# A two-row-block network on one core: the derived forms of h2 in three parts on VectorE, x transposed half a step earlier, a shorter Newton step

## The reference

```python
h  = s4d(log_dt, C=x, B, inv_A_real, A_imag, 1024)             # (32, 128, 1024)
h  = h  + layernorm(h)  @ attn_weight.T + attn_bias             # called h2 below
h2 = layernorm(h)
base = h2 @ W.T + b                                            # 1024 -> 1024
gates = softmax(h2 @ Wr.T)                                     # 4 experts
proj  = h2 @ A.T                                               # 4 experts x rank 8
out = h + base + sum over e of 2 * gates[e] * (proj[e] @ Bm[e].T)
```

## Time and profile before

| what | value |
|---|---|
| median of 3 runs | 901.78 us |
| the profiled execution, its own time | 901.64 us |
| its span (first to last instruction) | 899.7 us |
| TensorE (PE) busy | 85% of the span |
| VectorE (DVE) busy | 79% |
| ScalarE (ACT) busy | 66% |
| GpSimd (POOL) busy | 13% |

### The profile page before, as it was taken

How to read it: one execution, slowest core, us unless ns; L and a number is a source line. 1 busy time by engine, 2 the same in 40 slices (tenths; PEclk the granted TensorE clock), 3 DMA queues, 4 the chain that set the end, 5 groups by cost and what they waited for, 6 DMA issues and landing times.

```text
span 899.7 us, 15024 instructions
## 1 busy us (share of the span) xinstructions
PE 765.4 (85%) x5166; PEld 370.9 (41%) x5166; DVE 709.4 (79%) x1291; ACT 596.7 (66%) x979; POOL 118.3 (13%) x94
## 2 busy tenths in 40 slices
PE   2779999454989899898989899898989899898977
PEld 2624444222434344443434344343434344343433
DVE  7899996885987878787987878787987878787353
ACT  6778775665867677685777677685877677684120
POOL 2000202222020200202020200202020200202020
PEclk9979999886999999999989989899999999898999
DMA  8879676285243452526243452526243352526342
GB/s 295 247 143 172 148 160 130 72 186 101 51 93 82 83 111 50 123 50 141 54 95 77 82 111 50 122 50 140 55 91 81 82 111 50 117 50 129 51 93 62
DMA packets 258074, 94.21 MB, mean 105 GB/s; under 512 B 245424, under 2 KB 250416, under 8 KB 257912
## 3 DMA queue, kind: packets, MB, share of 16 engines
q1 hardware_dynamic: 257944, 93.66, 49.5%
q10 hardware_dynamic: 96, 0.13, 0.1%
HBM read 18.26 MB, written 16.78 MB: 39 GB/s over the span
## 4 chain that ended last, share of the span: by engine, by line
PE 43%; DVE 23%; ACT 9%; DMA 7%; issue 7%; SPq 7%; POOL 3%; DVEq 0%; POOLq 0%; ACTq 0%
PE ps_g L693 25%; PE ps_g L845 9%; PE ps_a L684 4%; DVE residual L1551 3%; DMA spare<-spare 3%; DVE u_split L1449 3%; SPq L524 2%; PE ps_x L845 2%; ACT junk L1047 2%; DVE form_tok L1879 2%; POOL form_sum L1400 2%; DVE residual L1886 2%; DMA forms<-form_tok 1%; SPq L511 1%; ACT form_tok L1230 1%
## 5 line engine op out<-in xcount | busy, mean ns | idle before, releaser
L693 PE MATMUL ps_g<-wa_hi,x 128*128 128x512 f16 x992 | 269.6, 388 | 7.3 <-DMA wa_lo<-residual 6.3
L693 PE MATMUL ps_g<-wa_lo,x 128*128 128x512 f16 x496 | 153.6, 389 | 0.0
L693 PEld LDWEIGHTS ps_g<-wa_hi,x 128*128 128x128 f16 x992 | 97.9, 100 | 130.5 <-issue 22.6
L684 PE MATMUL ps_a<-u_split,m_split 128*32 128x256 f16 x1344 | 58.1, 340 | 73.0 <-DVE u_split L1449 73.0
L845 PE MATMUL ps_g<-stage,forms 128*128 128x512 f16 x504 | 113.4, 379 | 7.1 <-DVE residual L1886 7.0
L1400 POOL TENSOR_TENSOR form_sum<-xn_b 128x512 f32<-128x512 f32 x14 | 18.1, 1290 | 581.0 <-DVE xn_b L1568 575.8
L684 PEld LDWEIGHTS ps_a<-u_split,m_split 128*32 128x32 f16 x1344 | 41.6, 117 | 92.2 <-issue 57.1
L845 PEld LDWEIGHTS ps_g<-stage,forms 128*128 128x128 f16 x504 | 48.5, 98 | 69.0 <-DVE residual L1886 9.3
L693 PEld LDWEIGHTS ps_g<-wa_lo,x 128*128 128x128 f16 x496 | 49.6, 100 | 61.8 <-issue 6.4
L1492 DVE TENSOR_TENSOR m<-x_t,q 128x512 f32<-128x512 f32 x32 | 22.0, 689 | 66.8 <-ACT x_t L1001 66.0
L1886 DVE SCALAR_TENSOR_TENSOR residual<-ps_g,unscale,residual 128x512 f32<-128x512 f32 x84 | 62.6, 745 | 14.7 <-PE ps_g L845 11.1
(11 more groups left out here) (273 smaller groups left out, 1450.2 us busy)
## 6 DMA issues: line engine op xcount, KB each, us to landing
out<-residual SPq DMA_DIRECT2D x124, 128.0 KB, 2.2
stage<-in_L_ffn_W SPq DMA_DIRECT2D x8, 512.0 KB, 14.0
x_raw<-in_x SPq DMA_DIRECT2D x38, 64.0 KB
residual<-in_L_attn_weight SPq DMA_DIRECT2D x4, 512.0 KB, 7.1
wf_hi<-in_x SPq DMA_DIRECT2D x1, 2048.0 KB, 9.4
xn_b<-in_L_ffn_W SPq DMA_DIRECT2D x4, 512.0 KB, 4.0
form_tok<-in_L_ffn_W SPq DMA_DIRECT2D x4, 512.0 KB, 5.4
forms<-form_tok SPq DMA_TRANSPOSE x106, 3.2
```

What stands on the lines that cost most here:

```text
L684: mm = pe.matmul(ps_a[q * C:(q + 1) * C, a // 2, (a % 2) * WL:(a % 2 + 1) * WL], stationary[:, q, a * C:(a + 1) * C], moving[:, q, :], sta ...
L693: mm = pe.matmul(ps[:, o, :], x1_part(part, ps is ps_g2)[:, k, :], ws[:, k, o * HALF:(o + 1) * HALF], start=k == 0 and part == 0 and ws is ...
```

## The change

Seven things are changed.

1. The four sums and differences go from GpSimd to VectorE: `add_first_form` (S1) right behind normalise_2(t, 1), `add_second_form` (S2) and `add_third_form` (S4) at the start of the next pair step, `add_fourth_form` (S3) behind its low_m. S3 is written to `form_sum`, no longer over `xn`.
2. The high parts, low parts and transposes of S2, S4 and S3 go into the next pair step. What is left at the end of a step is A22 and S1.
3. low_u(t + 1, 1) and high_u(t + 1, 1) now stand ahead of low A22 and high A22.
4. split_x(t + 2) goes ahead of square_2(t, 1), turn_x(t + 2) behind turn_x1(t + 1, 0), join_x(t + 2) ahead of phases and decays of (t + 2, 0); phases(t + 1, 1) goes ahead of square_2(t, 0).
5. `newton` has three operations, with eps multiplied by 1024 beforehand (one more operation once, at the start).
6. At the start split_x(3) and turn_x(3) go ahead of the second group of weight sums, and low_sums(3) ahead of keep_h2(2, 1).
7. At the end of the kernel the parts that were moved are written out behind the last step.

```diff
@@ SP, turn_second_forms and step
             def turn_second_forms(t):
                 turn_form(t, S1, 3, 2)
+                turn_form(t, A22, 2, 7)
+            def turn_third_forms(t):
                 turn_form(t, S2, 4, 3)
                 turn_form(t, S4, 5, 5)
-                turn_form(t, S3, 6, 6)
-                turn_form(t, A22, 2, 7)
...
             def step(t, p, stored=True, loads=True, turns=True):
-                if turns:
-                    turn_x(t + 1)
                 if stored:
                     store_pair(t - 2, 1, p)
                 if loads:
                     load_x(t + 2)
+                turn_third_forms(t - 1)
                 turn_x1(t, 1)
                 turn_pair_lora(t - 1)
+                turn_form(t - 1, S3, 6, 6)
                 turn_first_forms(t)
                 if turns:
                     turn_x1(t + 1, 0)
+                if loads:
+                    turn_x(t + 2)
                 store_pair(t - 1, 0, 1 - p)
                 turn_second_forms(t)
@@ ScalarE
                 rstd_guess(t, 1, stat_1, s_ssq1, s_log1, s_y1, m_eps)
+                if paired:
+                    high_form(t - 1, S2, 2)
+                    high_form(t - 1, S4, 3)
                 if waves:
                     high_m(t + 1, 0)
                 high_1(t, 1)
                 if waves:
                     sines(t + 1, 0)
+                    phases(t + 1, 1)
                 square_2(t, 0, p)
...
                     high_u(t + 1, 0)
+                if paired:
+                    high_form(t - 1, S3, 4)
                 high_first(t)
...
                     sines(t + 1, 1)
+                    if x:
+                        split_x(t + 2)
                 if sums:
                     high_sums(3)
                 square_2(t, 1, p)
                 rstd_guess(t, 1, stat_2, s_ssq2, s_log2, s_y2)
+                if waves:
+                    high_u(t + 1, 1)
                 high_form(t, A22, 0)
                 high_form(t, S1, 1)
-                high_form(t, S2, 2)
-                if waves:
-                    high_u(t + 1, 1)
-                high_form(t, S4, 3)
-                high_form(t, S3, 4)
+                if waves and x:
+                    join_x(t + 2)
+                    waves_ahead(t + 2, 0)
@@ GpSimd
-            add_forms(FIRST)
-            with pool.Fori(FIRST + 1, TILES) as t:
-                add_forms(t)
@@ VectorE, newton
-                dve.tensor_scalar(stat[:, 5:6], stat[:, 2:3], 1 / L, added, ALU.mult, ALU.add).then_inc(step_done, 1)
...
+                dve.tensor_scalar(stat[:, 5:6], stat[:, 2:3], added, stat[:, 4:5], ALU.add, ALU.mult)\
                     .then_inc(step_done, 1)
...
+                dve.tensor_scalar(stat[:, 6:7], stat[:, 5:6], stat[:, 4:5], -0.5 * XSCALE / L, ALU.mult, ALU.mult)\
                     .then_inc(step_done, 1)
...
+                dve.tensor_scalar(stat[:, 7:8], stat[:, 6:7], 1.5 * XSCALE, stat[:, 4:5], ALU.add, ALU.mult)\
+                    .then_inc(step_done, 1)
@@ VectorE, the new functions and pair_step
+            def add_first_form(t):
+                tau = t - FIRST
+                dve.wait_ge(s_xn2, 2 * t + 2)
+                if isinstance(t, int) and t == FIRST:
+                    dve.wait_ge(s_sum_t, 256)
+                else:
+                    dve.wait_ge(s_form_lo, LOWERED * tau)
+                dve.tensor_tensor(form_sum[:, :], xn_b[:, 0:HALF], xn_b[:, HALF:L], ALU.add).then_inc(s_form, 1)
+            def add_second_form(t):
...
+                dve.tensor_tensor(xn_b[:, 0:HALF], form_sum[:, :], xn[:, 0:HALF], ALU.subtract).then_inc(s_form, 1)
+            def add_third_form(t):
...
+                dve.tensor_tensor(xn[:, HALF:L], xn[:, HALF:L], xn_b[:, 0:HALF], ALU.subtract).then_inc(s_form, 1)
+            def add_fourth_form(t):
+                dve.wait_ge(s_form_lo, LOWERED * (t - FIRST) + 3)
+                dve.tensor_tensor(form_sum[:, :], xn_b[:, HALF:L], xn_b[:, 0:HALF], ALU.subtract).then_inc(s_form, 1)
...
             def pair_step(t, p, ended=True, following=True):
+                add_second_form(t - 1)
+                add_third_form(t - 1)
+                keep_h(t, 1)
                 if ended:
-                    keep_h(t, 1)
                     end_22(t - 2, p)
...
+                normalise_1(t, 1)
+                if following:
+                    round_turns(t + 1, 0)
+                low_form(t - 1, S2, 4)
+                low_form(t - 1, S4, 5)
+                low_1(t, 1)
+                if following:
+                    low_m(t + 1, 0)
+                add_fourth_form(t - 1)
                 keep_h2(t, 0, p)
...
                     low_u(t + 1, 0)
+                low_form(t - 1, S3, 6)
+                take_p5(t - 1, 1 - p)
                 low_first(t)
-                take_p5(t - 1, 1 - p)
                 take_p6(t - 1, 1 - p)
...
                 normalise_2(t, 1, p)
+                add_first_form(t)
                 end_12(t - 1, 1 - p)
+                take_p7(t - 1, 1 - p)
+                if following:
+                    low_u(t + 1, 1)
                 low_form(t, A22, 2)
                 low_form(t, S1, 3)
-                take_p7(t - 1, 1 - p)
-                low_form(t, S2, 4)
-                if following:
-                    low_u(t + 1, 1)
-                low_form(t, S4, 5)
-                low_form(t, S3, 6)
                 end_21(t - 1, 1 - p)
```

More of the change, by code:

```diff
@@ L154, in program @@
         m_power, m_mult, m_unscale, m_whole = (m_scale[:, k:k + 1] for k in range(4))
-        m_mean, m_eps, m_bias = (m_scale[:, k:k + 1] for k in range(4, 7))
+        m_mean, m_eps, m_bias, m_eps_sum = (m_scale[:, k:k + 1] for k in range(4, 8))
         x_all = wf_hi[:, :, :].rearrange("p a b -> p (a b)").bitcast(F32)
@@ L605, in _ @@
             turn_x2(1, 1)
+            turn_x(3)
             turn_sums(1)
             load_again(2)
-            turn_x(3)
             store(1, 0)
@@ L618, in _ @@
             turn_x1(3, 0)
+            turn_x(4)
             turn_sums(3)
@@ L642, in _ @@
             step(TILES - 1, 1, loads=False, turns=False)
+            turn_third_forms(TILES - 1)
+            turn_form(TILES - 1, S3, 6, 6)
             store_pair(TILES - 2, 1, 0)
@@ L1268, in first_half, with second_half @@
                     high_u(t + 1, 0)
+                if paired:
+                    high_form(t - 1, S3, 4)
                 high_first(t)
-            def second_half(t, p, waves=True, sums=False):
+            def second_half(t, p, waves=True, sums=False, x=True):
                 if waves:
@@ L1294, in _ @@
             step(1, 1, True)
+            split_x(3)
             high_sums(1)
-            split_x(3)
             waves_ahead(3, 0)
@@ L1300, in _ @@
             high_sums(2)
-            waves_ahead(3, 1)
+            decays(3, 1)
             second_half(2, 0, sums=True)
-            split_x(4)
-            waves_ahead(4, 0)
-            join_x(4)
             def pair_step(t, p):
                 first_half(t, p)
-                waves_ahead(t + 1, 1)
+                decays(t + 1, 1)
                 second_half(t, p)
-                split_x(t + 2)
-                waves_ahead(t + 2, 0)
-                join_x(t + 2)
             pair_step(3, 1)
@@ L1321, in _ @@
             first_half(t, 0)
-            waves_ahead(t + 1, 1)
-            second_half(t, 0)
+            decays(t + 1, 1)
+            second_half(t, 0, x=False)
             t = TILES - 1
@@ L1326, in _ @@
             second_half(t, 1, waves=False)
+            high_form(t, S2, 2)
+            high_form(t, S4, 3)
+            high_form(t, S3, 4)
             pair_exp(t)
@@ L2042, in _ @@
             next_h(3, 0, 2, 1, True)
+            low_sums(3)
             keep_h2(2, 1, 0)
             make_u(3, 1)
-            low_sums(3)
             normalise_2(2, 1, 0)
+            add_first_form(2)
+            low_u(3, 1)
             low_form(2, A22, 2)
             low_form(2, S1, 3)
-            low_form(2, S2, 4)
-            low_u(3, 1)
-            low_form(2, S4, 5)
-            low_form(2, S3, 6)
             pair_step(3, 1, ended=False)
@@ L2061, in _ @@
             end_22(t - 1, 0)
+            add_second_form(t)
+            add_third_form(t)
+            low_form(t, S2, 4)
+            low_form(t, S4, 5)
+            add_fourth_form(t)
+            low_form(t, S3, 6)
             take_p1(t, 1)
```

57 lines of the change are left out of this document (19 added, 38 removed).

## The result

The changed kernel takes 799.33 us (median of 4 runs, 798.64 to 801.72), beside 901.57 us (900.99 to 902.13) for the kernel before in the same runs: a ratio of 0.887, interval 0.885 to 0.889. Run again beside the experiments it took 799.95 us, 0.8874 (0.8862 to 0.8887). The profiled execution took 801.72 us with a span of 799.9.

What follows compares the result with a forecast made beforehand. TensorE was taken to bound the kernel, pausing for a late low_u and restarting slowly. From the 899.7 us span, 14 (start), 76.7 (steps) and 7.8 (tail) leave 801.2; with 1.9 around it 803 us, range 794 to 835.

Steps and rivals of the forecast that it cites:

- Start: Before the steps: earlier turn_x(3) saves 10 us, earlier low_u(3, 1) saves 4; together 14 us, bounds 4 and 16.
- Twelve steps: 12 pair steps of 44.1 us plus one slow restart of 2.4: 531.6 us in place of 608.3, 76.7 less.
- Tail: Behind the last step: slow restart of s4(15, 1) and product_2(15)'s wait for end_21 go; 7.8 us less, bounds 3 and 10.
- The floor of 43.9 us: TensorE's unchanged work in one pair step at full clock, without the pause ahead of s4: 43.9 us, against 50.70.
- The chain to low_u: VectorE from keep_h2(t, 1) to low_u's end, without GpSimd: s4 could follow at 615.7, so TensorE's 4.39 us pause shrinks to 0.1.
- x earlier: In the steps: VectorE's wait for x_t (66.0 us in all) goes, but lies beside TensorE's attn and shortens nothing by itself.
- GpSimd: Sums moved to VectorE add 2.8 us a step; ended stretching by GpSimd gives back 1.1 on low_u, 1.9 on three forms.
- R3: Rival: SP's order delays x1(t, 1), so TensorE waits before attn(t, 1) each step; slower, 903 us at the limit; chance 0.03.
- R1: Rival: VectorE and ScalarE become the bound through waits for ScalarE; steps of 46 or 47 us, 833 us; chance 0.20.
- R2: Rival: small stalls of 0.1 to 0.5 us each bring a slow restart and keep TensorE's clock low; 832 us; chance 0.08.
- R4: Rival: low_u still 2 us late for a missed reason, pause and restart partly stay; steps of 48.5 us, 856 us; chance 0.10.
- The start's order on SP: SP's queue: same DMAs reordered, turn_third_forms(t - 1) ahead of turn_x1(t, 1), about 5 us to spare in a step.

## Why the prediction was right, and where its reasons were not

*Terms.* The span was forecast as 801.2 and is 799.9 in the profile. Start: 14 forecast, 13.9 in this profile and 16.0 in that of the second run. Its two parts: TensorE's wait for the lora transpose went from 11.27 to 1.89, 9.4 against the forecast 10, and the wait for low_u(3, 1) from 20.30 to 16.63, 3.7 against 4. Twelve steps: 531.6 forecast, 531.1 measured. Tail: 7.8 forecast, 8.7 measured. The floor of 43.9 us, put together from pieces of the earlier trace rows, is the term that carried the prediction, and the runs with split_x behind square_2 show it bare: 43.82.

*The chain to low_u.* Forecast to be 0.1 late, and 0.1 to 0.3 more for split_x ahead of square_2; measured 0.34 to 0.44, and nothing without split_x there. s4(t, 1) takes 1.50 and low_u 1.22, as said. The newton term was sized too small: 0.25 for one operation counted once, where the loop holds four at 0.19 and 0.77 us a step came out. The slow restart behind the start was there (199.75, 2.75 us).

*x earlier.* Here a step failed. The prediction said that the wait for x_t "has been beside TensorE's attn, so it frees VectorE and shortens nothing by itself". Putting x back late costs 43 us. VectorE's list runs from x_t through make_m, round_turns, low_1, low_m, keep_h2(t, 0), make_u and normalise_2(t, 0) to take_p1, on which product_6 waits. In the kernel before this second loop was almost as long as the first: the 0.85 us ahead of the product at 643.15 is its mark, and such pauses, 0.35 to 1.68 us, stand in eight of the twelve steps. The forecast called take_p1 "as late as before" and yet kept 0.1 of the 0.85, without a reason; measured it comes 2.5 us sooner behind s4(t, 1) (19.67, not 22.18), and 0.3 us in time. So the sum was right at this place by luck: it gave x no share, and would have been the same with x left late, where 843 us were measured. No run moves x alone in the kernel before, so "by itself" is open there.

*GpSimd.* The stretching is real (1.75 beside GpSimd, 0.68 not), and 3.0 us won (1.1 on low_u, 1.9 on three forms) for 2.8 added is nearly an even trade in the prediction's own sum. With everything else changed, the run shows no difference; the trade alone, with the forms together as before, was not run. The prediction says that the rows agree with the rule that it names only in kind, since low_u lost 1.1 us and "not a whole second run". That is misread: the loss is what was left of GpSimd's instruction (last section), and so the rows agree in size too.

*What did.* Neither part is a share of 102 us. Low_u ahead alone, in the kernel before: 30 us slower. Low_u behind two forms, in the changed one: 13 us slower. Forms split over two steps: 90. x early: 43. These add up to more than the change, which fits two loops of nearly one length that go through the same queues: to shorten one is worth nothing, or less, until the other is short too. That low_u first makes the kernel slower with the rest as before was in no rival of the prediction. It isn't the forms alone: with low_u first and the forms together, but x early, the shorter newton and the start as changed, it took 891.08 us, 11 less than the kernel before. R3 came nearest, since its place (what SP turns late) was near, but its price was not asked for at product_6.

*The rivals.* R1 (VectorE bounds): wrong in size, not in kind. VectorE has 4.4 us idle in 44 (its load is 39.6 in that stretch; the idle time before was over 9 us a step, not the 8 of the prediction), and its loop with ScalarE takes 44.2 us against TensorE's 43.8, not 46 to 47; but it is this loop that sets the step, as the run with the four-operation newton shows, until split_x leaves it. R2 (small stalls keep the clock low): refuted, ten pauses of 0.32 to 0.47 us with s4 at 1.49 to 1.52. The Trainium skill (TensorE: Matmul & The Clock Gate, "Part 1: The HAM clock gate") warns of micro-idles; no run here shows a fall of the clock behind pauses of up to 1.68 us. R3: product_6 waits, not attn for x1: for more than 0.5 us only where forms or x are late. R4: refuted.

*The start's order on SP* was called harmless for the steps, which it is (12 steps, no wait for x1). That the same line of code runs at t = 2 with the weight sums in between, where moving one ScalarE operation costs some 8 us, was not seen; it hit an experiment, not the prediction.

## What to carry to other kernels

Build the floor of the bounding engine from uncontended rows of its own timeline, and then ask for every chain that ends on it, not only for the one with the visible wait: a small pause elsewhere (0.85 us here) can be the mark of a second loop that takes over as soon as the first is shortened. Where loops are of nearly one length, parts of a change can't be priced one by one against the kernel before; take each one out of the finished version as well. On an in-order queue put what the bounding engine waits for first, and what only has to be done by the next round last.

## What the runs showed of the hardware that was not expected

Behind a pause TensorE came back at full speed or not, and the length of the pause didn't decide it alone. Behind 0.32 to 1.24 us s4 took 1.49 to 1.61 us (1.60 and 1.61 also stand where there is no pause). In the kernel before, behind 1.67 and 1.68 us twelve matmuls of 512 columns took 2.75 and 2.76, as without a pause. With x late, three pauses of 2.87, 2.89 and 2.92 us were followed by 2.76, but another of 2.89 by 5.30, about double, and one of 2.64 by 4.45; 2.97 to 3.34 us were followed by 4.09 to 4.33, and 3.60 by 5.30. The granted clock was 1.00 from 415.4 to 418.0 and 0.50 from 701.96 to 707.2, behind pauses of the same length:

```profile
415.42 2.76 PE L852 MATMUL ps_g<-stage,forms 128*128 128x512 f16 x12 [2.89 <-DVE residual L1911]
...
701.96 5.30 PE L852 MATMUL ps_g<-stage,forms 128*128 128x512 f16 x12 [2.89 <-DVE residual L1911]
```

Longer pauses aren't followed by a longer slow stretch: 5.3 to 5.6 us by 4.55 to 5.08 (forms together), 7.2 to 7.6 us by 4.07 to 5.30 (low_u alone). The runs with x late also spread the most, by 8 us (839.33 to 847.26); that this is the clock is likely, not shown.

VectorE and GpSimd did not slow each other evenly: where a sum of GpSimd met low_u or a low form of VectorE, the one that began first kept its length, and the other ended a set time behind its end. In the kernel before, GpSimd's sum of 617.25 ends at 618.96, and low_u, begun at 617.76, ends 1.08 us behind it, having 1.22 when alone. With the sums on GpSimd in the changed kernel low_u begins first, at 641.36, and keeps its 1.22; the sum of 641.44 takes 2.27, where one that meets nothing of the kind takes 1.27 (640.10). The low form begun at 642.49 then ends 0.55 us behind that sum, having 0.68 when alone:

```profile
617.25 1.71 POOL L1406 TENSOR_TENSOR xn<-xn_b 128x512 f32<-128x512 f32 x1
```

```profile
641.44 2.27 POOL L1418 TENSOR_TENSOR xn_b<-form_sum,xn 128x512 f32<-128x512 f32 x1
```

So each loses what is left of the other's instruction, less about 0.14 us, and which of them loses goes by who begins; low_u was 0.08 us ahead. A low form that waited for a whole sum lost 1.07 us (1.75, not 0.68); the length of GpSimd's own row, 1.27 to 2.27, holds its waiting too and is no measure of it.
